# Two short causal score blocks in one PSUM bank, with their masks joined

## The reference

```python
def _L0_attn_ref(x, w_q, w_kv, w_dense):          # x is layer-normed; 16 heads, 4 groups, 128 per head
    q = jnp.einsum('bsh,he->bse', x, w_q).reshape(b, sq, GROUPS, HPG, KVC)
    ...
    scores = jnp.einsum('bqgpd,bkgd->bgqpk', q, k) * (SCALE / LAYER_INDEX)
    causal = jnp.arange(sq)[:, None] >= jnp.arange(sk)[None, :]
    scores = jnp.where(causal[None, None, :, None, :], scores, -jnp.inf)
    probs = jax.nn.softmax(scores, axis=-1).astype(x.dtype)
    ctx = jnp.einsum('bgqpk,bkgd->bqgpd', probs, v).reshape(b, sq, HEADS * KVC)
    return jnp.einsum('bse,eh->bsh', ctx, w_dense)
```

## Time and profile before

| what | value |
|---|---|
| median of 3 runs | 2766.25 us (2765.52 to 2767.22) |
| the profiled execution | 2764.28 us, span 2762.5 us |
| mean granted TensorE clock | 0.984 |
| TensorE busy (matmuls) | 2645.2 us, 96% of the span |
| VectorE / ScalarE / GpSimd busy | 2151.4 / 934.7 / 883.2 us |
| attention on TensorE | from about 873 us to 1927 us |
| score products, matmuls | 1536, 324.4 us |
| mask matmuls of the attention (L1231) | 512, 230 ns each on the record |

### The profile page before, as it was taken

One profiled execution on the slowest core, in us unless ns is written; L12 is line 12 of the kernel. 1 busy time (PEld: TensorE's weight loads), 2 busy tenths in 40 slices (PEclk: granted clock), 3 DMA queues, 4 the chain that ended last, 5 costly groups with the idle time before them and its releaser, 6 DMA issues. The chain is left out here.

```text
span 2762.5 us, 47188 instructions
## 1 busy us (share of the span) xinstructions
PE 2645.2 (96%) x15460; PEld 2404.3 (87%) x15460; DVE 2151.4 (78%) x5550; ACT 934.7 (34%) x2560; POOL 883.2 (32%) x1944
## 2 busy tenths in 40 slices
PE   6999999999994999999999999998899999999998
PEld 5999999999993888888888888887799999999997
DVE  5888888888875777777777777776788888888887
ACT  3111101111003766666767666665311110111010
POOL 3332333233220333343434343433432332323321
PEclk8999999999997999999999999999899999999999
DMA  6000000000002433333333333334300000000000
GB/s 183 1 1 1 1 1 1 1 1 1 1 1 86 87 77 87 77 87 77 87 77 87 77 87 77 87 77 91 108 1 9 9 1 9 9 1 9 9 9 8
DMA packets 378739, 117.37 MB, mean 42 GB/s; under 512 B 338560, under 2 KB 377472, under 8 KB 378496
## 3 DMA queue, kind: packets, MB, share of 16 engines
q1 hardware_dynamic: 378496, 114.36, 17.7%
HBM read 26.24 MB, written 4.19 MB: 11 GB/s over the span
## 5 line engine op out<-in xcount | busy, mean ns | idle before, releaser
L444 PE MATMUL ffn_ring<-ffn_mix_weights,ffn_yT 128*128 128x384 f32 x6144 | 1248.2, 345 | 16.0 <-DVE ffn_mix_weights L672 8.4
L444 PEld LDWEIGHTS ffn_ring<-ffn_mix_weights,ffn_yT 128*128 128x128 f32 x6144 | 1085.8, 191 | 60.4 <-issue 8.5
L611 DVE SCALAR_TENSOR_TENSOR ffn_mix_sums<-ffn_ring,ffn_w,ffn_mix_sums 128x384 f32<-128x384 f32 x896 | 550.4, 615 | 243.8 <-PE ffn_ring L444 224.3
L1481 POOL CAST attn_probsT<-attn_turned 128x1024 fp32r<-128x1024 f16 (+3 forms) x512 | 347.9, 721 | 594.5 <-DVE attn_probs L1343 592.1
L495 PE MATMUL ffn_ring<-ffn_out_weights,ffn_avT 128*128 128x512 f32 x1536 | 440.5, 398 | 3.3 <-POOL ffn_avT L903 3.3
L1196 PE MATMUL attn_scores<-attn_kT,attn_qT 128*128 128x256 f32 (+2 forms) x1536 | 324.4, 338 | 20.3 <-ACT attn_exponentials L1417 17.9
L1417 ACT ACTIVATE attn_exponentials<-attn_scores,attn_score_neg_max 128x512 f32<-128x512 f32 (+3 forms) x512 | 268.2, 528 | 164.1 <-DVE attn_score_neg_max L1327 163.1
L1327 DVE TENSOR_REDUCE attn_score_neg_max<-attn_scores 128x1 f32<-128x512 f32 (+3 forms) x512 | 246.5, 485 | 82.0 <-PE attn_scores L1231 73.7
L495 PEld LDWEIGHTS ffn_ring<-ffn_out_weights,ffn_avT 128*128 128x128 f32 x1536 | 283.1, 189 | 29.2 <-POOL ffn_avT L903 4.6
L1196 PEld LDWEIGHTS attn_scores<-attn_kT,attn_qT 128*128 128x128 f32 x1536 | 243.7, 191 | 41.6 <-ACT attn_exponentials L1417 21.2
L1196 PE MATMUL attn_ctx<-attn_probsT,attn_v 128*128 128x256 f32 (+2 forms) x1536 | 269.0, 324 | 0.0
(11 more groups left out here) (134 smaller groups left out, 2720.8 us busy)
## 6 DMA issues: line engine op xcount, KB each, us to landing
ffn_mix_stage<-in_L_ffn_q_proj_dram SPq DMA_DIRECT2D x32, 128.0 KB, 2.6
ffn_mix_stage<-in_L_ffn_k_proj_dram SPq DMA_DIRECT2D x32, 128.0 KB, 2.6
ffn_mix_stage<-in_L_ffn_v_proj_dram SPq DMA_DIRECT2D x32, 128.0 KB, 3.0
ffn_out_stage<-in_L_ffn_o_proj_dram SPq DMA_DIRECT2D x16, 256.0 KB, 3.2
attn_turned<-attn_probs SPq DMA_TRANSPOSE x256, 3.4
out_dram<-x SPq DMA_DIRECT2D x8, 512.0 KB, 3.0
x<-in_L_attn_x_dram SPq DMA_DIRECT2D x7, 512.0 KB, 7.8
attn_weight_stage<-in_L_attn_w_q_dram SPq DMA_DIRECT2D x4, 512.0 KB, 8.0
```

What stands on the lines that cost most here:

```text
L444: last = pe.matmul(bank[:, 0:QKV], yT[:, t % 2, h, k * P:(k + 1) * P], wm[:, e, wh, k], start=(n == 0), stop=(n == 3 * CK - 1))
L611: dve.scalar_tensor_tensor(into, bank[:, 0:QKV], w[:, t, e:e + 1], into, ALU.mult, ALU.add).then_inc(mix_done, 1)
L1481: pool.tensor_copy(cast(i), landed(n, i).rearrange("p (j h q) -> p j h q", h=HL, q=P)).then_inc(t_cast, 1)
```

## The change

Three things in the attention, and a name. (1) Blocks 1 and 0 share one bank, `sc[2]`: block 1 in its columns 0 to 255, block 0 in columns 256 to 511, of which the first 128 count. Only block 1's first matmul starts the bank. (2) Their diagonal parts, columns 128 to 255 and 256 to 383, lie side by side and get their masks by one 256-wide matmul, from a tile that holds the mask twice; it signals for both. (3) The masks of blocks 3 and 2 come one after the other behind the products of block 2. With the banks go the waits: block 3 waits for block 3 of the unit before, block 1 for block 0 of the unit before, block 0 for nothing; the exponential of block 1 waits for the maxima of both short blocks. GpSimd copies the mask once at the start of the attention, and TensorE waits for that.

```diff
-        pool.memset(m.mask[:], 0.0).then_inc(filled, 1)
+        pool.memset(m.mask2[:, 0], 0.0).then_inc(filled, 1)
...
-        pool.affine_select(out=m.mask[:], in_=m.mask[:], compare_op=ALU.is_ge, fill=MASKED, base=0,
+        pool.affine_select(out=m.mask2[:, 0], in_=m.mask2[:, 0], compare_op=ALU.is_ge, fill=MASKED, base=0,
...
-                pe.matmul(sc[:, t * P:n], m.ident_bf[:], m.mask[:], start=False, stop=True).then_inc(scores_ready, 1)
+                pe.matmul(sc[:, t * P:n], m.ident_bf[:], m.mask2[:, 0], start=False, stop=True).then_inc(scores_ready, 1)
...
-        zeroed = sem("zeroed")
+        zeroed, masks_made = sem("zeroed"), sem("masks_made")
...
         def scores_bank(i):
 
-            return sc[turn_of(i) % (QT - 1)]
+            return sc[turn_of(i)][:] if i else sc[QT - 2][:, 2 * P:]
...
-                reach(pe, e_done, done_of(n, QT - 1) if i == 0 else done_of(n - 1, 0 if i == QT - 1 else i))
+                if i:
+                    reach(pe, e_done, done_of(n - 1, i if i > 1 else 0))
                 width = max(i + 1, 2) * P
                 product(scores_bank(i)[:, 0:width], lambda a: qT[:, h % 2, a, i * P:(i + 1) * P],
-                        lambda c: kT[:, h // PER, c, 0:width], True, False)
-                pe.matmul(scores_bank(i)[:, i * P:(i + 1) * P], m.ident_bf[:], m.mask[:], start=False, stop=True,
+                        lambda c: kT[:, h // PER, c, 0:width], i > 0, False)
+
+            def mask_long(i):
+
+                pe.matmul(scores_bank(i)[:, i * P:(i + 1) * P], m.ident_bf[:], m.mask2[:, 0], start=False, stop=True,
                           skip_group_check=True).then_inc(s_ready, 1)
+
+            def mask_short():
+
+                pe.matmul(sc[QT - 2][:, P:3 * P].rearrange("p (a k) -> p a k", k=P), m.ident_bf[:], m.mask2[:],
+                          start=False, stop=True, skip_group_check=True).then_inc(s_ready, 2)
...
                     scores(now, 3)
                     scores(now, 2)
+                    mask_long(3)
+                    mask_long(2)
                 place("B")
                 if now:
                     scores(now, 1)
                     scores(now, 0)
+                    mask_short()
                 place("C")
...
+            pe.wait_ge(masks_made, 1)
             for n, what in enumerate(PROLOGUE):
...
-                act.wait_ge(s_max, done_of(n, i))
+                act.wait_ge(s_max, done_of(n, 0 if i == 1 else i))
...
+            pool.tensor_copy(m.mask2[:, 1], m.mask2[:, 0]).then_inc(masks_made, 1)
             for half in range(HL):
...
-        m.mask = sb("causal_mask", [P, P], BF16)
+        m.mask2 = sb("causal_mask_pair", [P, 2, P], BF16)
```

## The result

| | median us (runs) | ratio to before [95% interval] |
|---|---|---|
| first measurement | 2739.18 (2734.37 to 2740.53, 4) | 0.9897 [0.9881, 0.9912] |
| measured again, a0_changed | 2737.0 (2735.04 to 2739.08, 4) | 0.9903 [0.9888, 0.9918] |
| measured again, a1_changed | 2737.62 (2734.59 to 2741.97, 4) | 0.9904 [0.9887, 0.992] |

The change makes the kernel 27 to 29 us faster. The forecast was 31 less by the profiled execution, and 2735 us. The first profiled execution took 2739.33 us (before: 2764.28).

A forecast was written before the change was run, and what follows sets the result against it. TensorE's stream was taken to bound the ordinary slot. Terms over 128 slots sum to 31.2 us, taking the profiled 2764.28 to 2733.1, as a median 2735; the forecast's own range is 2730 to 2740, with rivals 2728 to 2752.

The forecast's parts named there:

- 89 ordinary slots: Attention slots without the removed wait: cheaper masks save 0.18 us each, 16.0 us in all.
- head 12, seven items: Dense products start earlier, then context products wait for the last cast: gain 0.60 us each, 4.2 in all.
- head 14, seven items: Second z transpose waits for a q split that comes 0.28 us later: loss 2.0 us in all.
- heads 1 and 2 of the first item: Where the chains fill at the start of the attention: gain 0.6 us, an estimate.
- head 0, first item's included: Second value projection follows the q split, whose chain doesn't move, so the 0.18 us is eaten: gain 0.
- What one mask costs, and the masks after: TensorE's stream: a mask costs 0.12 us, four 0.48; afterwards 0.06, 0.12 and wide 0.12, sum 0.30, saving 0.18 a slot.
- Rival 1: Masks don't get cheaper, pair and wide mask cost what four did: gain 14 us, 2752; chance 0.09.
- Waits removed: Block 0 no longer waits for block 3's exponential: gains 0.71 us in head 3, 0.60 in head 12, 1.05 in head 15.
- Waits added: Later maxima delay VectorE's q split by 0.28 us: head 14 loses 0.28, head 0 gains 0, elsewhere nothing lost.
- Rival 2: Cover runs out: VectorE, ScalarE and casts bound the short slots; gain 18 us, 2748; chance 0.14.
- Rival 3: Block 3's maximum, 0.53 us later, delays context products in every slot: 37 us slower, 2803; chance 0.04.
- No change at all: The whole kernel's time stays the same; a difference under 5.5 us can't be told from none; chance 0.03.

The follow-up runs named there:

- a0_changed: The changed kernel unaltered, measured again beside the kernel before: 2737.0 us, ratio to before 0.9903.
- a1_changed: The changed kernel unaltered, measured once more, on another chip: 2737.62 us, ratio to before 0.9904.
- e4_two_narrow: The changed kernel with the wide mask of blocks 1 and 0 as two 128-wide masks in a row, one signal: 2740.15 us, ratio to before 0.9908.
- e3_wait_back: The changed kernel with block 0 waiting again for the exponential of block 3 of its own unit: 2755.54 us, ratio to before 0.9968.
- e5_ctx_first: The changed kernel with VectorE splitting the context ahead of block 3's maximum in all heads: 2738.97 us, ratio to before 0.9899.
- e7_combined: e6_early_q plus, in head 3 alone, the context split ahead of the first maximum: 2727.41 us, ratio to before 0.9858.
- e6_early_q: The changed kernel; heads 0 and 14 split q before short maxima and block 2's exponential, head 14 also z splits: 2731.23 us, ratio to before 0.987.
- e2_short_only: The changed kernel with each long mask behind its own product again; shared bank and wide mask kept: 2742.43 us, ratio to before 0.9927.
- e1_pair_only: The kernel before with only the masks of blocks 3 and 2 in a row; old banks, waits and short masks: 2763.54 us, ratio 0.9996.
- e9_all_early: e7_combined with the q projection split early in every head from 0 to 13: 2731.65 us, ratio to before 0.9878.

## Why the prediction was right

By its own steps, as the slots of the first profiled execution show them (gain times count, us):

| term | forecast | measured |
|---|---|---|
| 89 ordinary slots | 0.18: 16.0 | 0.16: 14.4 |
| head 3, seven items | 0.71: 5.0 | 0.73: 5.1 |
| head 12, seven items | 0.60: 4.2 | 0.48: 3.4 |
| head 15, seven items | 1.05: 7.4 | 1.03: 7.2 |
| head 14, seven items | -0.28: -2.0 | -0.28: -2.0 |
| heads 1 and 2 of the first item | +0.6 | -0.2 |
| head 0, first item's included | 0 | -0.3 |
| sum | 31.2 | 27.6 |

The mechanism was right in its main parts: a cheaper mask, a wait removed, and what is late next. Two readings were not: that the stream behind the masks stays as it is, and that it is the shared bank that costs heads 14 and 0. What the runs leave to explain is the 3.6 between the sums.

- **What one mask costs, and the masks after.** Median distances in the trace after: from the pair's first mask to its second 0.066 (forecast 0.06), from the first to the product behind both 0.095, and from that to the next 0.315, where a free 512-wide one takes 0.233. So the pair costs 0.095 + 0.082 = 0.177, 0.18 forecast. Wide mask 0.122, 0.12 forecast. Four masks cost 0.49 before, so 0.19 is saved in these distances (0.18 forecast). Rival 1 is out. (The rule of the Trainium skill that I weighed, "TensorE: Matmul & The Clock Gate", section "Back-to-back issue gap", would have the first mask at 0.08; 0.066 was measured.)
- **The mis-sized term is the ordinary slot**, 0.16 instead of 0.18 (0.14 in heads 4 to 6). The prediction took the stream behind the masks as unchanged. It isn't: the 18 matmuls from the first dense product to the first context product of head 5 took 2.14 before, and take 2.21 after (1303.35 to 1305.56), unrounded 0.057 more. That is the wider spacing of the 256-wide ones, and it is the whole difference between the 0.19 that the masks save and the 0.14 of this slot. e4_two_narrow has the old spacing in most slots and e3_wait_back, with the wide mask, in some: the width of the mask isn't the cause, and the cause stays open.
- **Head 12.** Both forecast times were met within 0.01 (the cast's signal took 0.05 where 0.08 was allowed, a term that none of the rows shows). The 0.12 that is missing stands behind them: the context product's first weight load waits for the last cast and is no longer hidden, and the product's record is 0.50 long, not 0.39. The prediction stopped at the start of that product.
- **Waits removed.** e3_wait_back puts the wait back alone, and 18 us go. It isn't the prediction's 16.6 measured again: that was the gain of three heads over the kernel before, 15.7 measured. In heads 3 and 12 the context split was late next, as forecast (head 3's context products came at 5.61, forecast 5.65; the 1.4 and 0.7 that stand beside that figure make only 5.54, but nothing hangs on it). e5_ctx_first and e7_combined remove that wait, and head 3 gains 0.48 more. In head 12 the cast is late behind it, as forecast too.
- **Waits added.** Head 14's z transpose waited 0.69 (forecast some 0.7), and head 0's value projection 0.33. e6_early_q takes both away and gains 0.71 and 0.39 there, so a change of order buys back these waits, and with them the 0.24 that head 14 waited before. The prediction put this price on the shared bank. That is half right: e2_short_only, which shares the bank, costs head 14 0.25 and head 0 its gain, but e1_pair_only, with the old banks, costs them 0.28 and the gain as well. Either part makes the q split late, and both together hardly more than one. The rule of the Trainium skill on rotating banks ("Perfetto Trace Analysis", section "Matmuls") is borne out as far as e2_short_only shows it: sharing costs in 2 heads of 16, and gains in the others.
- **First item.** The 0.6 was an estimate. Head 1 gained 0.57, but at head 2 the scores wait 1.90 for the q split, and the clock falls behind it (TensorE's timeline; then the window from 898 to 902, clock 0.57):

```profile
897.14 1.64 PE L1196 MATMUL attn_scores<-attn_kT,attn_qT 128*128 128x512 f32 x6 [1.90 <-DVE attn_qT L1333]
...
898.77 2.91 PE L1196 MATMUL attn_projections<-attn_zT,attn_wq 128*128 128x512 f32 x6
```

```profile
898.00:902.00 4.00, 4.00 (x16) 3.15 (x15) 3.10 (x6) 2.24 (x7) 1.38 (x2) 0.57 0.42 95
```

The six projections of 512 columns take 2.71 us (898.77 to 901.48) instead of 1.48, as in head 5. In a0_changed the same wait is there and the clock stays at 1.00 from 896 to 900, and the item gains 0.8 more. So this 0.8 belongs to the execution, not to the change. The wait itself is there in both (0.91 for another split before), and the estimate had left it out: that heads 1 and 2 gain 0.59 in a0_changed, as forecast, is luck.
- **Rival 2**, the cover runs out: the casts end 1.75 before the context products in head 5 (1303.81 against 1305.56). They stand where they stood in the slot, 3.31 behind its start, so that only the shorter slot was lost of the 1.88 before, not the 0.46 that I allowed. In heads 8, 9, 10 and 13 it is mostly 0.56 to 0.93, forecast some 0.7; head 8 had 0.74 before already, not the 1.2 of the prediction, and lost less. No ordinary slot waits, and e9_all_early, which delays the short blocks further, makes none of them wait for a cast. The cover holds, down to 0.5 us in head 13 there.
- **Rival 3**: e1_pair_only has the delay without the shared bank and isn't slower.
- **No change at all** is out by the intervals.

The rest between the slots and the time: in the first execution the attention as a whole ends 28 us earlier and the span is 25 shorter, by the half-clock stretch behind the attention; in a0_changed the span is 29 shorter (2733.2). The forecast of the profiled time, 2733.1, is 6.2 below the first execution's 2739.33 and 1.9 below a0_changed's 2735.04; how near it comes depends on the execution.

## What to carry to other kernels

Price a short instruction in a dense stream by the distance between starts, with the late start of the second product behind it (read here as a weight load that isn't hidden): a 128-column mask was 0.12 us, half of what its record says, and putting two in a row halved the first. Then look again at the stream behind it, since its pace can change with the order. Sharing a bank removes the wait for the bank's old reader and adds one for the later of two writers. Ask who needs the work queued behind these readers (the q split here), since its delay, whatever part of the change brings it, was the loss; it was bought back by moving splits ahead in two of 16 heads. Moving the q split in all heads, or the context split in all heads without asking the same question, gained nothing.

## What the runs showed of the hardware

- Identical streams of 256-wide float32 matmuls ran at two spacings at the full clock, 113 to 114 ns or 118 ns, for the rest of the dense and value products. Head 5 has 118 in the changed kernel and 113 to 114 in e3_wait_back behind the same 256-column mask, and head 12 of the kernel before has 118 behind a 128-column one. No run shows what sets it.
- A bf16 mask of 256 columns costs what one of 128 costs (0.122 and 0.123 us): 0.04 to the next start in both, and 0.08 by which the second float32 product behind it starts late. With another mask behind it, one of 128 takes 0.066.
- After the same wait of 1.9 us in the first item the clock fell to 1.2 GHz in some executions (the first and a1_changed) and not in others (a0_changed); it costs 0.8 us there. The half-clock time behind the attention differs by 6 us between the first execution and a0_changed, and that part is 2.7 us longer.
